# Experts' rows added into two accumulators by the transfers themselves, in place of a row for every token and expert

## The reference

```
scores  = softmax(x @ gate_w.T)                    # 1088 x 64
idx     = top_k(scores + gate_b, 6)                # 6 of 64 experts for each token
xb[e]   = the rows of x routed to expert e, at most 128
h       = silu(xb @ w1.T) * (xb @ w3.T)            # 176 wide, for each expert
yb      = h @ w2.T                                 # 128 x 256 for each expert
y[tok] += yb[e, pos] * scores[tok, e]              # at most 6 addends a token
z       = silu(x @ ws1.T) * (x @ ws3.T) @ ws2.T    # the shared expert
out     = x_before_norm + y + z
```

## Time and profile before

| | |
|---|---|
| median of 3 runs | 669.67 us (668.56 to 670.07) |
| profiled execution, its time | 671.24 us |
| its span from first to last instruction | 669.3 us |
| PE busy | 523.9 us, 78% |
| PE weight load | 444.4 us, 66% |
| DVE busy | 446.8 us, 67% |
| ACT busy | 370.0 us, 55% |
| POOL busy | 234.2 us, 35% |
| TensorE clock granted, mean | 0.897 |
| chain that ended last, by engine | PE 45%, DVE 29%, DMA 7%, issue 7%, POOL 5%, ACT 5% |

### The profile page before, as it was taken

How to read it: one execution, slowest core, us unless ns; L and a number is a source line. 1 busy time by engine, 2 the same in 40 slices (tenths; PEclk the granted TensorE clock), 3 DMA queues, 4 the chain that set the end, 5 groups by cost and what they waited for, 6 DMA issues and landing times.

```text
span 669.3 us, 9768 instructions
## 1 busy us (share of the span) xinstructions
PE 523.9 (78%) x3182; PEld 444.4 (66%) x3182; DVE 446.8 (67%) x928; ACT 370.0 (55%) x899; POOL 234.2 (35%) x235
## 2 busy tenths in 40 slices
PE   3945954266735989999999997696999999998945
PEld 3723843133313989999999885585888888787834
DVE  5949897999998245644454613475787887776516
ACT  1637645345545647667676443444777776676600
POOL 2021001023424311011111203157777777777710
PEclk9975988578766989999999999797999999999969
DMA  8960000018000000000000001001777776776466
GB/s 276 383 240 0 1 0 0 0 35 289 5 1 0 24 1 25 24 24 25 25 1 1 1 1 48 21 26 47 204 227 220 211 226 188 220 215 196 123 249 226
DMA packets 44053, 67.43 MB, mean 101 GB/s; under 512 B 11149, under 2 KB 27142, under 8 KB 43876
## 3 DMA queue, kind: packets, MB, share of 16 engines
q1 hardware_dynamic: 36836, 64.62, 30.2%
q0 software_dynamic: 7168, 2.20, 1.8%
HBM read 66.81 MB, written 17.72 MB: 126 GB/s over the span
## 4 chain that ended last, share of the span: by engine, by line
PE 45%; DVE 29%; DMA 7%; issue 7%; POOL 5%; ACT 5%; SPq 1%; POOLq 0%; DVEq 0%; ACTq 0%
PE ps L711 6%; PE ps L712 6%; PE ps L713 6%; PE ps L922 5%; PE ps L1058 5%; PE ps L880 4%; DVE region L1700 3%; DMA region<-y_rows 2%; PE ps L911 2%; DMA y_rows<-region 2%; POOL y_rows L678 2%; PE ps L894 2%; PE ps L1033 2%; DVE region L1644 2%; DMA region<-x_rows,region 2%
## 5 line engine op out<-in xcount | busy, mean ns | idle before, releaser
L1700 DVE TENSOR_TENSOR region<-ps,region 32x136 f32<-32x136 f32 x128 | 38.1, 297 | 73.3 <-PE ps L880 71.8
L711 PE MATMUL ps<-nTh,high 128*128 128x272 f32 (+2 forms) x248 | 75.1, 303 | 12.3 <-ACT region L1277 8.7
L678 POOL DMA_INDIRECT y_rows<-region x64 | 71.4, 1116 | 21.6 <-issue 12.8
L669 POOL DMA_INDIRECT region<-x_rows,region x64 | 71.5, 1117 | 20.7 <-issue 15.8
L712 PE MATMUL ps<-nTl,high 128*128 128x272 f32 (+2 forms) x248 | 72.8, 294 | 0.0
L632 POOL COPY region<-region 32x544 f32<-32x544 f32 x32 | 26.1, 814 | 133.4 <-DVE region L1719 131.9
L1058 PE MATMUL ps<-region 88*128 88x256 f32 x256 | 65.6, 378 | 0.0
L1830 DVE TENSOR_TENSOR w_low<-region,high 128x704 fp32r<-128x704 f32 x64 | 56.7, 886 | 4.5 <-ACT high L1366 4.4
L711 PEld LDWEIGHTS ps<-nTh,high 128*128 128x128 f32 (+2 forms) x248 | 47.1, 190 | 15.1 <-ACT region L1277 10.3
L713 PE MATMUL ps<-nTh,pairs_low 128*128 128x272 f32 x192 | 55.9, 291 | 0.0
L1366 ACT ACTIVATE high<-region 128x704 fp32r<-128x704 f32 x64 | 50.1, 783 | 0.0
(11 more groups left out here) (247 smaller groups left out, 1369.5 us busy)
## 6 DMA issues: line engine op xcount, KB each, us to landing
region<-moe_w SPq DMA_DIRECT2D x64, 352.0 KB, 3.8
region<-moe_w SPq DMA_DIRECT2D x64, 176.0 KB
y_rows<-zrow SPq DMA_DIRECT2D x1, 6528.0 KB, 25.4
region<-y_rows SPq DMA_DIRECT2D x8, 768.0 KB, 9.9
region<-wqkv SPq DMA_DIRECT2D x8, 384.0 KB, 3.0
region<-ffn_w SPq DMA_DIRECT2D x2, 1024.0 KB, 8.2
region<-patches SPq DMA_DIRECT2D x3, 384.0 KB, 8.2
region<-patches SPq DMA_DIRECT2D x1, 1152.0 KB, 10.7
```

The source lines that it names most:

```text
L669: nc.gpsimd.indirect_dma_start(out=xb[m8], out_offset=None, in_=x_rows, in_offset=bass.IndirectOffsetOnAxis(ap=sloti[:, m8:m8 + 1], axis=0 ...
L678: nc.gpsimd.indirect_dma_start(out=y_rows, out_offset=bass.IndirectOffsetOnAxis(ap=sld[m8], axis=0), in_=yb[m], in_offset=None, bounds_che ...
L711: nc.tensor.matmul(out, parts_a[0], parts_b[0], start=first, stop=False)
L1700: last = V.tensor_tensor(sc[r, s0:s0 + 8, 0:T].rearrange("p (a b) t -> p a b t", a=4), ps[r, 4:8, 0:4 * GW].rearrange("p a (b h t) -> p a ...
```

## The change

y_rows becomes two accumulators with one row for each token (2 x 1088 rows). put adds: experts of even number into the first, of odd number into the second, with the token's own number as the row. An adding transfer must not overlap another one into the same rows, so put(e) now waits for the landing of put(e-2). The row numbers of a put are the ones of its gather, so `sloti` keeps 16 experts and its writer (keep_slots) waits for the landing of older puts; L1845, s_sld, the scan, `nth`, `first` and the 32 words a row behind the probabilities go. Six transfers read the accumulators back, and DVE adds them to h in two adds a chunk; PE has no part in the sums.

```diff
-XW = D + E + E // 2
+XW = D + E
-        nth = reg2.cut([P, NT, E])
-        first = reg2.cut([P, NT, E])
-        sloti = reg2.cut([P, EB]).bitcast(U32)
-        sld = [reg2.cut([P, 1]).bitcast(U32) for _ in range(EB)]
+        sloti = reg2.cut([P, 2 * EB]).bitcast(U32)
-        picked = reg2.cut([P, NT, TOPK * D])
+        picked = [reg2.cut([P, NT, D]) for _ in range(2)]
-        y_rows = nc.dram_tensor("y_rows", (N * TOPK + 1, D), F32, kind="Internal").ap()
+        y_rows = [nc.dram_tensor(f"y_rows{k}", (N, D), F32, kind="Internal").ap() for k in range(2)]
...
-            sp.dma_start(y_rows[1:, :].rearrange("(p r) d -> p r d", p=P), bc(zrow[:, :], 1, N * TOPK // P)).then_inc(s_yzero, 16)
+            for k in range(2):
+                sp.dma_start(y_rows[k].rearrange("(p r) d -> p r d", p=64), bc(zrow[0:64, :], 1, N // 64)).then_inc(s_yzero, 16)
...
-            for t in range(NT):
-                sp.dma_start(picked[0:rows(t), t, :],
-                             y_rows[1 + TOPK * P * t:1 + TOPK * (P * t + rows(t)), :].rearrange("(p k) d -> p (k d)", k=TOPK)
-                             ).then_inc(s_back[t // 2], 16)
+            for c, (a, b) in enumerate(CHUNKS):
+                for k in range(2):
+                    sp.dma_start(tiles(picked[k], a, b), token_rows(y_rows[k], a, b)).then_inc(s_back[c], 16)
...
-            nc.gpsimd.memset(first, 1.0).then_inc(s_xbz, 1)
...
-            nc.gpsimd.memset(first[:, :, 0:1], 0.0).then_inc(s_xbz, 1)
...
             def gather(e, b, m8):
+                at = EB * (b % 2) + m8
                 m = m8 % 4
                 pool.wait_ge(s_tab, 2 * b + 1 + m8 // 4)
                 need(pool, s_xtb, e - 7)
-                need(pool, s_sld, e - 7)
+                need(pool, s_eh, e - 7)
                 need(pool, s_got[m], 4 * (e - 4 - m) + 16)
...
             def put(e, m8):
-                m = m8 % 4
+                m, at = m8 % 4, e % (2 * EB)
                 pool.wait_ge(s_yb, e + 1)
-                pool.wait_ge(s_sld, e + 1)
+                need(pool, s_add[(m + 2) % 4], 4 * (e - 2 - (m + 2) % 4) + 16)
                 nc.gpsimd.indirect_dma_start(
-                    out=y_rows, out_offset=bass.IndirectOffsetOnAxis(ap=sld[m8], axis=0), in_=yb[m], in_offset=None,
-                    bounds_check=last_row, oob_is_err=False).then_inc(s_add[m], 16)
+                    out=y_rows[e % 2], out_offset=bass.IndirectOffsetOnAxis(ap=sloti[:, at:at + 1], axis=0), in_=yb[m],
+                    in_offset=None, bounds_check=last_token, oob_is_err=False, compute_op=ALU.add).then_inc(s_add[m], 16)
...
-            for t in range(1, NT, 2):
-                pe.wait_ge(s_back[t // 2], 32)
-                for k in range(TOPK):
-                    mm = nc.tensor.matmul(ps[:, t // 2, 0:D], ident[:, :], picked[:, t, k * D:(k + 1) * D],
-                                          start=(k == 0), stop=(k == TOPK - 1))
-                mm.then_inc(s_sum, 1)
...
-            link(V.tensor_tensor_scan(nth.rearrange("p t e -> p (t e)"), first.rearrange("p t e -> p (t e)"),
-                                      selb.rearrange("p t e -> p (t e)"), 0.0, ALU.mult, ALU.add))
-            V.tensor_copy(nth16, nth).then_inc(s_xpk, 1)
...
-                V.tensor_scalar(sloti[:, 4 * half:4 * half + 4], slotf[:, cs], 0.0, None, ALU.add).then_inc(s_tab, 1)
+                to = EB * (q % 2) + 4 * half
+                for e in range(at - 2 * EB + 2, at - 2 * EB + 4):
+                    need(dve, s_add[e % 4], 4 * (e - e % 4) + 16 if e >= 0 else 0)
+                V.tensor_scalar(sloti[:, to:to + 4], slotf[:, cs], 0.0, None, ALU.add).then_inc(s_tab, 1)
...
-                    need(dve, s_add[m], 4 * (n - 8 - m) + 16)
-                    dve.wait_ge(s_slot, b + 1)
-                    V.scalar_tensor_tensor(out=sld[m8], in0=slot_of(slotf, n), scalar=float(TOPK),
-                                           in1=slot_of(xb[m8].bitcast(BF16), 2 * (D + E) + n), op0=ALU.mult,
-                                           op1=ALU.add).then_inc(s_sld, 1)
...
-            for t in range(NT):
-                r = slice(0, rows(t))
-                if t % 2:
-                    dve.wait_ge(s_sum, t // 2 + 1)
-                    V.tensor_tensor(h[r, t, :], ps[r, t // 2, 0:D], h[r, t, :], ALU.add).then_inc(s_fin, 1)
-                else:
-                    dve.wait_ge(s_back[t // 2], 16 * min(2, NT - t))
-                    p = picked[r, t, :].rearrange("p (k d) -> p k d", k=TOPK)
-                    link(V.tensor_tensor(p[:, 0:3, :], p[:, 0:3, :], p[:, 3:6, :], ALU.add))
-                    link(V.tensor_tensor(p[:, 0, :], p[:, 0, :], p[:, 1, :], ALU.add))
-                    link(V.tensor_tensor(h[r, t, :], h[r, t, :], p[:, 2, :], ALU.add))
-                    V.tensor_tensor(h[r, t, :], h[r, t, :], p[:, 0, :], ALU.add).then_inc(s_fin, 1)
+            for c, (a, b) in enumerate(CHUNKS):
+                dve.wait_ge(s_back[c], 32)
+                link(V.tensor_tensor(tiles(h, a, b), tiles(h, a, b), tiles(picked[0], a, b), ALU.add))
+                V.tensor_tensor(tiles(h, a, b), tiles(h, a, b), tiles(picked[1], a, b), ALU.add).then_inc(s_fin, b - a)
```

More of the change, by code:

```diff
@@ L405, in build @@
         s_h4 = sem("s_h4")
-        s_sld = sem("s_sld")
         s_got = sems("s_got", 4)
@@ L432, in build @@
         s_slot = sem("s_slot")
-        s_back = sems("s_back", 5)
-        s_sum = sem("s_sum")
+        s_back = sems("s_back", 3)
         s_fin = sem("s_fin")
@@ L639, in _ @@
             pool.wait_ge(s_proj, NT)
-            nc.gpsimd.memset(first, 1.0).then_inc(s_xbz, 1)
             for j in range(EB):
                 nc.gpsimd.memset(xb[j], 0.0).then_inc(s_xbz, 1)
-            pool.wait_ge(s_xbz, 9)
-            nc.gpsimd.memset(first[:, :, 0:1], 0.0).then_inc(s_xbz, 1)
             nc.gpsimd.tensor_copy(spread_e, bc(ident[0:E, 0:E], 2, SG)).then_inc(s_xbz, 1)
             nc.gpsimd.iota(code, [[-1, N]], SKIP, 0, allow_small_or_imprecise_dtypes=True).then_inc(s_xbz, 1)
-            pool.wait_ge(s_xbz, 12)
+            pool.wait_ge(s_xbz, 10)
             nc.gpsimd.memset(hsh[96:128, 2, :], 0.0).then_inc(s_xbz, 1)
-            pool.wait_ge(s_xbz, 13)
+            pool.wait_ge(s_xbz, 11)
             for k in range(3 * CH):
@@ L656, in _ @@
             pool.wait_ge(s_xrow, 16 * (NT + 2))
-            pool.wait_ge(s_yzero, 16)
+            pool.wait_ge(s_yzero, 32)
             last_token = pool.to_reg(N - 1)
-            last_row = pool.to_reg(N * TOPK)
             def gather(e, b, m8):
+                at = EB * (b % 2) + m8
                 m = m8 % 4
@@ L666, in gather @@
                 need(pool, s_xtb, e - 7)
-                need(pool, s_sld, e - 7)
+                need(pool, s_eh, e - 7)
                 need(pool, s_got[m], 4 * (e - 4 - m) + 16)
                 nc.gpsimd.indirect_dma_start(
-                    out=xb[m8], out_offset=None, in_=x_rows, in_offset=bass.IndirectOffsetOnAxis(ap=sloti[:, m8:m8 + 1], axis=0),
+                    out=xb[m8], out_offset=None, in_=x_rows, in_offset=bass.IndirectOffsetOnAxis(ap=sloti[:, at:at + 1], axis=0),
                     bounds_check=last_token, oob_is_err=False).then_inc(s_got[m], 16)
             def put(e, m8):
-                m = m8 % 4
+                m, at = m8 % 4, e % (2 * EB)
                 pool.wait_ge(s_yb, e + 1)
-                pool.wait_ge(s_sld, e + 1)
+                need(pool, s_add[(m + 2) % 4], 4 * (e - 2 - (m + 2) % 4) + 16)
                 nc.gpsimd.indirect_dma_start(
-                    out=y_rows, out_offset=bass.IndirectOffsetOnAxis(ap=sld[m8], axis=0), in_=yb[m], in_offset=None,
-                    bounds_check=last_row, oob_is_err=False).then_inc(s_add[m], 16)
+                    out=y_rows[e % 2], out_offset=bass.IndirectOffsetOnAxis(ap=sloti[:, at:at + 1], axis=0), in_=yb[m],
+                    in_offset=None, bounds_check=last_token, oob_is_err=False, compute_op=ALU.add).then_inc(s_add[m], 16)
             def pool_step(n, b, m8):
@@ L1004, in place_slots @@
                                  start=True, stop=True).then_inc(s_tabps, 1)
-            pe.wait_ge(s_xbz, 12)
+            pe.wait_ge(s_xbz, 10)
             pe.wait_ge(s_group, 1)
@@ L1370, in act_step @@
                         act.wait_ge(s_hsh, 3 * CH)
-                        act.wait_ge(s_xbz, 13)
+                        act.wait_ge(s_xbz, 11)
                     need(act, s_z, t)
@@ L1747, in _ @@
             logits = ps[:, 4:6, :].rearrange("p a b -> p (a b)")[:, 0:NT * E].rearrange("p (t e) -> p t e", e=E)
-            prob, nth16 = xpk[:, :, 0:E], xpk.bitcast(BF16)[:, :, 2 * E:3 * E]
+            prob = xpk[:, :, :]
             link(V.tensor_reduce(gmx, logits, AX.X, ALU.max))
@@ L1754, in _ @@
             link(V.tensor_tensor(prob, lg, bc(gsum, 2, E), ALU.mult))
-            link(V.tensor_tensor(rank, prob, bc(gate_b, 1, NT), ALU.add))
+            V.tensor_tensor(rank, prob, bc(gate_b, 1, NT), ALU.add).then_inc(s_xpk, 1)
```

(12 more changed lines are left out.)

2 lines of the change are left out of this document (removed).

## The result

The changed kernel takes **690.33 us** (median of 4 runs, 687.53 to 692.16) beside 669.12 us of the kernel before (4 runs, 668.09 to 670.07): ratio 1.0328, 95% interval 1.0289 to 1.0368. It is slower by 21.2 us; the prediction was +12.4 and 682 us, with 657 to 712 as its range. The profiled execution is the quickest of these four, 687.53 us with a span of 684.5.

The account below looks back on a forecast made before the run. POOL's full transfer queue was taken to set the loop's second half, with PE nearly full. Wait +25, start -2.0, tail -12.4 and last put +1.8 made +12.4 us on the median 669.67: 682 us, range 657 to 712.

Parts of the forecast that it names:

- Part 1, issue: Puts in the expert loop: making them adding leaves their issue time on POOL unchanged, 0, at most +0.5 us a put.
- rival (B): Puts on POOL: the issue itself grows by 0.3 to 0.5 us each, giving 697 us (688 to 715); chance 0.20.
- Part 1, landing and wait: Expert loop: adding puts land in 5.7 us, and waiting for the put two experts back costs 62 x 0.4 = +25 us.
- POOL pays in full: Expert loop, second half: POOL's queue sets the pace without slack, so anything holding it is paid in full.
- Part 2: Expert loop: removed L1845 instructions on DVE, narrower gather rows and an earlier semaphore for the gather change nothing, 0.
- Part 3: Gating stage: dropping the scan and cast from DVE only lengthens its idle time, 0; up to 2 us could come.
- Part 4: Start of the kernel: a smaller zero fill shortens POOL's library change before rstd, -2.0 us, between 0 and -2.8.
- Part 5: Tail: fewer, smaller reads and sums gain 12.4 us, against +1.8 us for the last put's longer landing and wait.

Follow-up runs that it names:

- the eight kinds of put: Changed kernel with experts taking turns between adding and plain puts of 128 rows, 64 rows, 128 half rows and 32 rows: 676.25 us, one run.
- The wait alone: Kernel before, with each put also waiting for the landing of the put two experts back, nothing adding: 671.85 us, ratio 1.0050.
- the run with adding alone: Kernel before with its puts made adding, no wait added: 708.34 us, ratio 1.0577; in another set of runs 703.03 us, ratio 1.0145.
- second batch: Follow-up runs of four altered kernels beside the kernel before, which took 668.40 us; the changed kernel with plain puts took 657.64 us, ratio 0.9823.
- third batch: Follow-up runs beside the kernel before at 696.15 us: changed kernel 691.61 us, with plain puts 683.33 us, with four accumulators 690.39 us.

## Why the prediction was right in sign and wrong in its main step

**Part 1, issue: wrong.** This is the step that failed. The prediction took 0 for the added issue, since gather and put of unlike bytes and direction had the same one, and +0.5 us as its end; the measured value is +0.57, above that end. That two transfers of unlike bytes and direction cost the same said nothing of a third kind with an operation in it, and the eight kinds of put show why the comparison misled: neither bytes nor, for the most part, rows set the issue, but the kind of the instruction. A price without a row had deserved the middle of its bounds; 64 x 0.25 = 16 us would have stood in the sum. This was rival (B), at a chance of 0.20, and it is the mechanism found: 1.59 us of issue where it said 1.3 or more. Its price of 697 us was too high because it kept some 14 us of waiting beside the issue, and there was none.

**Part 1, landing and wait: wrong in size.** Taken: landing 5.7 us, wait 25 us. Measured: landing 4.2 us, and no put that POOL held back for one. The landing behind the issue did not grow (2.7 and 2.6 us), so the 2.0 us set down for reading the rows do not show at all. The wait alone costs 3.4 us with plain puts and nothing that can be told with adding ones. The two errors stood against each other, 25 us for the wait in place of 31 us for the issue. That a wrong mechanism gave 682 us where 690 were measured is luck.

**POOL pays in full: right.** The reading of the loop, a queue that is full at 0.79 busy because of the 0.30 us between transfers, carries the whole result. By the medians 64 puts and gathers would take 37.7 us more (0.57 and 0.02 each); POOL's account says 32.9, because the time that its occasional longer transfers add to their medians fell from some 12 us to 7. The loop took 31.1 more, so next to none of it was hidden: the idle time before the transfers fell by only 1.1 us.

**Part 2: right** as a cost of 0. In the run with adding alone, which still has L1845, POOL's profile names it in 12 idle times before a put, 3.7 us in all; that is 0.3 us each, the usual gap, so it held nothing. From the first put to the last that run takes 208.8 us and the changed kernel 201.6, since its two kinds of transfer take 184.4 us in all in place of 175.8, with medians as in the changed kernel (1.59 us the put, 1.04 the gather). Why more of its transfers are long is not shown, and L1845 was not left out by itself.

**Part 3: right.** The scan's time became idle time, 3.65 us ahead of the instruction that takes PE's counts, in place of 1.46 ahead of L1772 in the earlier trace rows:

```profile
439.44 1.28 DVE L1753 TENSOR_SCALAR region<-ps 64x1088 f32<-64x1088 f32 x1 [3.65 <-PE ps L979]
```

**Part 4: wrong**, -2.0 predicted, 0 measured. The stretch ahead of rstd is 7.65 us with DMA at rest, 7.55 with the fill under way. The 9.90 us of the first library change, under load, had been read as the effect of load; the second shows no such effect. The Trainium skill, GPSIMD Engine Reference, section 2.1 Instruction dispatch, gives 5.95 us for the load of a freshly loaded kernel; both stretches here lie above it, and what else they hold is not shown.

**Part 5: right.** Predicted 12.4 less 1.8 for the last put, so 10.6; measured 12.15 behind the last put's start. The last landing, 666.49 + 2.7 = 669.2 at the shortest, stands 15.3 us ahead of the end, where 15.5 was written down; an add of 1024 columns takes 1.23 us (1.22 predicted). The +1.8 was too much: a landing without load went from 2.1 to 2.7, and no wait for expert 61 shows.

## What to carry to other kernels

A queue is full when its transfers and the gaps between them fill the time, whatever its busy share says; before a change puts a new kind of instruction on such a queue, measure that instruction's own duration, since a neighbour of like size is no price for it. On GpSimd an adding indirect transfer takes 1.5 to 1.6 times as long to issue as a plain one and hardly longer to land, so it pays where POOL has slack or the queue carries few of them, and not in a loop at POOL's bound. Where the aim is fewer bytes in the tail and the results bear it, narrow the rows first: rows of bf16 left the loop alone and gained 7.6 us.

## What the runs showed of the hardware that was not expected

The surcharge of adding is mostly fixed (441 ns at 32 rows, 591 at 128), hardly changes with the bytes of a row (563 at half rows), and comes with 96 nearly empty packets for each put. The Trainium skill, DMA: Bandwidth & Descriptors, section Anatomy of one DMA, calls descriptor generation small and variable and gives most of a transfer's fixed time to the write receipt; here the part on the engine, 1.02 and 1.59 us, is what decides, and the landing behind it, 2.6 us, costs nothing.

The second finding is the 26 us between batches. From the first put to the last, the kernels with plain puts took 170.5 us (before, in the trace at the head), 172.8 (after with plain puts, second batch) and 200.2 (the same kernel, third batch); the changed kernel took 201.6, and in the third batch 204.5. The put line of the changed kernel with plain puts in the third batch, and two windows of that run (columns as above):

```profile
L671 POOL DMA_INDIRECT y_rows<-region x64: 980/1022/1588, 466.5 to 666.6; - x64
...
521.00:522.00 1.00, 0.00 (x0) 0.00 (x0) 0.41 (x1) 0.22 (x1) 0.00 (x0) 1.00 0.03 2
522.00:523.00 1.00, 0.11 (x1) 0.11 (x2) 0.56 (x2) 0.92 (x3) 0.00 (x0) 1.00 0.00 0
```

The puts are as short as ever, but the loop has stops of some 2 us, like this one, in which PE, POOL and the DMA engines have almost nothing to do, and which the trace puts down to another core or an unknown queue. POOL is no busier with its transfers (140.0 us in all, 141.4 in the second batch) but idles 28.6 us more before them (74.8 and 46.2), nearly all of it waiting for ACT's L1330, and ACT's own waits that the profile puts down to "remote" come to over 30 us, where the second batch has none. So this loop runs at 3.18 us an expert where it otherwise takes 2.74. A loop with adding puts, at 3.23 us by POOL's own queue, hardly notices. Hence the sign of this change depends on the batch: 1.0328 where the kernel before takes 669 us, 0.9939 (0.9909 to 0.9969) where it takes 696. What the stops are stays open. All three batches ran on the same chip, and the kernel before is the same program in each, so neither of the two explains the difference between them, though the expectations above speak of another chip; the kernel before was not traced in the slower batches. The comparison that the prediction was made for is the first.
